# One meeting of the engines between six stages instead of two, with the finished stage's semaphores cleared inside the next stage and Pool's queue not drained

## What is computed

```
x = x + 0.5 * moe(layernorm(x))          # 8 experts, the best 2 of each token, hidden width 256
x = x + attention(layernorm(x))          # 16 heads of 16, rotary, causal softmax
x = x + 0.5 * moe(layernorm(x))          # the same weights again
x = x + 0.5 * hadamard_ffn(layernorm(x)) # fwht(silu(x W1) * (x W3)) W2, hidden width 1024
x = x + feature_attention(layernorm(x))  # sin and cos of random projections in place of the softmax
x = x + 0.5 * hadamard_ffn(layernorm(x))
```

## Time and profile before

| | us |
|---|---|
| median of 3 runs | 1163.23 |
| the runs | 1161.66 to 1166.33 |
| span of the profiled execution | 1142.1 |
| median less span | 21.1 |

### The profile page before, as it was taken

One profiled execution on the slowest core, in us unless ns is written; L12 is line 12 of the kernel. 1 busy time (PEld: TensorE's weight loads), 2 busy tenths in 40 slices (PEclk: granted clock), 3 DMA queues, 4 the chain that ended last, 5 costly groups with the idle time before them and its releaser, 6 DMA issues. The chain is left out here.

```text
span 1142.1 us, 18339 instructions
## 1 busy us (share of the span) xinstructions
PE 1029.9 (90%) x6327; PEld 844.4 (74%) x6327; DVE 732.0 (64%) x1755; ACT 449.2 (39%) x768; POOL 430.7 (38%) x473
## 2 busy tenths in 40 slices
PE   4889995879999999978999987999988998899997
PEld 3778884756566655568878886888877987788886
DVE  7935442899788876647454445756648978456654
ACT  4324331327576654525343322232325543232222
POOL 3046663337363721203556531000129987300000
PEclk8689998889899997896999998999998999999999
DMA  9024422400000010119452241000010120000000
GB/s 335 37 74 139 171 88 83 128 0 2 2 2 20 2 39 20 39 37 352 149 189 89 79 174 53 1 1 1 1 74 1 28 47 1 1 1 19 20 19 19
DMA packets 39339, 72.49 MB, mean 63 GB/s; under 512 B 10642, under 2 KB 28114, under 8 KB 38996
## 3 DMA queue, kind: packets, MB, share of 16 engines
q1 hardware_dynamic: 29460, 48.25, 12.6%
q0 software_dynamic: 7680, 20.98, 5.6%
q10 hardware_dynamic: 2112, 2.10, 0.5%
HBM read 47.04 MB, written 24.13 MB: 62 GB/s over the span
## 5 line engine op out<-in xcount | busy, mean ns | idle before, releaser
L2139 PE MATMUL ps<-xt,w 128*128 128x512 f32 x768 | 191.3, 399 | 7.5 <-PEq L66 7.5
L2139 PEld LDWEIGHTS ps<-xt,w 128*128 128x128 f32 x768 | 142.4, 191 | 37.0 <-issue 5.8
L1822 DVE CUSTOM_DVE_ANT_0 ps<-ps,att_mask 128x128 f32<-128x128 f32 (+3 forms) x256 | 119.2, 515 | 27.2 <-PE ps L1371 26.9
L717 PE MATMUL ps<-moe_w,moe_narrow_xb 128*128 x480 | 127.6, 402 | 0.0
L2233 DVE TENSOR_TENSOR had_gated<-ps,had_sig 128x512 f32<-128x512 f32 x64 | 44.2, 691 | 109.7 <-ACT had_sig L2192 109.7
L2192 ACT ACTIVATE had_sig<-ps 128x512 f32<-128x512 f32 x64 | 38.2, 597 | 188.4 <-PE ps L2139 188.4
L1679 ACT ACTIVATE att_early_probs<-ps 128x384 f32<-128x384 f32 (+1 forms) x192 | 91.2, 528 | 52.1 <-PE ps L1386 51.5
L122 POOL TENSOR_TENSOR var_eps<-bn,eps 128x4 f32<-128x4 f32 x24 | 6.6, 274 | 277.0 <-DVE bn L99 263.0
L621 POOL DMA_INDIRECT made_rows<-moe_units_made,moe_index x80 | 79.4, 993 | 80.4 <-ACT moe_units_made L844 68.3
L615 POOL DMA_INDIRECT moe_xs<-xn_rows,moe_index x80 | 79.3, 991 | 76.0 <-DVE moe_index L1016 44.1
L717 PEld LDWEIGHTS ps<-moe_w,moe_narrow_xb 128*128 128x128 f32 x480 | 92.0, 192 | 20.2
(11 more groups left out here) (286 smaller groups left out, 2242.8 us busy)
## 6 DMA issues: line engine op xcount, KB each, us to landing
moe_w<-in_moe SPq DMA_DIRECT2D x16, 768.0 KB, 8.9
back<-made_rows SPq DMA_DIRECT2D x16, 512.0 KB, 5.4
x<-x_turned SPq DMA_DIRECT2D x8, 512.0 KB, 8.6
low_weights<-moe_w SPq DMA_DIRECT2D x4, 768.0 KB, 3.6
moe_w<-low_weights SPq DMA_DIRECT2D x4, 768.0 KB, 15.2
x<-in_x SPq DMA_DIRECT2D x4, 512.0 KB, 5.5
xn_rows<-moe_wide_xn SPq DMA_DIRECT2D x4, 512.0 KB, 10.6
moe_narrow_later<-in_w SPq DMA_DIRECT2D x4, 512.0 KB, 4.6
```

Source lines behind the costliest of these rows:

```text
L717: last = nc.tensor.matmul(h_bank(j, i), xb[a][:, j % 2, i, k, :], weight(c), start=False, stop=(k == KC - 1 and c == 1))
L1822: last = nc.vector.tensor_tensor_reduce(g.ps[:, a, col:col + n], g.ps[:, a, col:col + n], mask[:, SEQ - n:SEQ], -1.0, 3.0e38, ALU.add, ALU ...
L2139: last = nc.tensor.matmul(g.ps[:, bank(n, half), :], w[a][:, k, c * P:(c + 1) * P], xt[low][:, b % 2, k, :], start=(k == 0 and q == 0), st ...
```

## The change

A stage no longer clears its semaphores when it ends. It hands the list on, and the next stage has it cleared by Pool after the one meeting that is left, ahead of Pool's list of that stage. That list is allocated while the old one is still held, so semaphores which only one of the two experts stages uses are now made in that one alone. `no_gpsimd_drain=True` takes Pool's own drain out of the meeting. In had0 Pool waits for its two weight subtractions before it leaves the stage. After the last stage nothing is cleared.

```
 class Semaphores:
+    finished = []
     def __init__(self, nc, ctx, tag):
         self.nc, self.tag, self.held = nc, tag, []
-        ctx.callback(self.clear)
+        ctx.callback(self.hand_on)
...
-    def clear(self):
-        self.nc.clear_and_free_semaphores(self.held)
-        self.nc.all_engine_barrier()
+    def hand_on(self):
+        Semaphores.finished.append(self.held)
+
+    def clear_finished(self):
+        while Semaphores.finished:
+            self.nc.clear_and_free_semaphores(Semaphores.finished.pop())
...
         # in each of the four stage functions
-        block = ctx.enter_context(nc.Block())
+        sem.clear_finished()
+        block = ctx.enter_context(nc.Block(no_gpsimd_drain=True))
...
         # hadamard_stage, Pool's list
-                    nc.gpsimd.tensor_tensor(w[1][:, :, :], raw[:, :, :], f32(w[0][:, :, :]), ALU.subtract)
+                    nc.gpsimd.tensor_tensor(w[1][:, :, :], raw[:, :, :], f32(w[0][:, :, :]), ALU.subtract) \
+                        .then_inc(raw_low, 1)
+                pool.wait_ge(raw_low, 2)
```

More of the change, by code:

```diff
@@ L464, in experts_stage @@
         later = narrow("later", [P, HID])
-        consts, small_here, b2_here = sem("consts"), sem("small_here"), sem("b2_here")
+        b2_here = sem("b2_here")
+        if which == 0:
+            consts, small_here, xn_stored, pool_const = sem("consts"), sem("small_here"), sem("xn_stored"), sem("pool_const")
         x_here = [sem(f"x_here{b}") for b in range(BATCH)]
         rec_here = [sem(f"rec_here{e}") for e in range(E)]
-        low_here = [sem(f"low_here{e}") for e in range(E)]
-        low_stored = sem("low_stored")
+        if which == 1:
+            low_here = [sem(f"low_here{e}") for e in range(E)]
+        if which == 0:
+            low_stored = sem("low_stored")
         LOADED = E // 2 if which == 1 else 0
         b1_here, b1_filled = sem("b1_here"), sem("b1_filled")
[L473 to L476, removed]
+        hi_split, lo_split, zeroed = sem("hi_split"), sem("lo_split"), sem("zeroed")
+        if which == 0:
+            gate_split, both_done = sem("gate_split"), sem("both_done")
+        if which == 1:
+            route_turned, rows_out, rows_stored, route_here = (
+                sem("route_turned"), sem("rows_out"), sem("rows_stored"), sem("route_here"))
         routed, margin_done, route_done, chosen_done = (
@@ L481, in experts_stage @@
         b1_turned, b_hi, b_row = sem("b1_turned"), sem("b_hi"), sem("b_row")
-        xn_stored = sem("xn_stored")
         gathered = [sem(f"gathered{s}") for s in range(AHEAD)]
@@ L501, in experts_stage @@
             jobs += split(g.w1, "w1")
-        w3_here, w3_hi, mixed, w2_hi = sem("w3_here"), sem("w3_hi"), sem("mixed"), sem("w2_hi")
+        if which == 1:
+            w3_here, w3_hi, mixed, w2_hi = sem("w3_here"), sem("w3_hi"), sem("mixed"), sem("w2_hi")
         later_here, later_hi, later_lo = sem("later_here"), sem("later_hi"), sem("later_lo")
@@ L2050, in hadamard_stage @@
             raws = [sb("lqkv_raw", [P, KC, 2 * D]), sb("lout_raw", [P, KC, D])]
-        raw_here, raw_hi = sem("raw_here"), sem("raw_hi")
+        raw_here, raw_hi, raw_low = sem("raw_here"), sem("raw_hi"), sem("raw_low")
         rope_here, bias_here, blocks_here = sem("rope_here"), sem("bias_here"), sem("blocks_here")
```

## The result

The changed kernel takes 1157.38 us (median of 12 runs, 1155.20 to 1161.63); the kernel before 1165.11, in 12 runs too. The ratio is 0.9940, with a 95% interval from 0.9922 to 0.9958: 7.0 us less, and 4.9 to 9.1 by the interval. The forecast time of 1157.5 us was met, but in part by luck: the gain was forecast as 5.7 us against a median of 1163.23, and its main assumption, a long drain behind the meeting, did not hold.

The account below looks back on a forecast made before the run. PE, busy for 90% of the span, bounds most of a stage, so only seams could move. Terms of 0.6 + 0.9 + 2.9 + 0.5 + 0.5 + 0.5 - 0.2 = 5.7 us off 1163.2 gave 1157.5 us, range 1153.8 to 1161.5.

Parts of the forecast that it names:

- The second meeting: At each seam, dropping it saves 1.1, 0.9, 1.0, 0.5, 0.5 us, fea to had1 taken at 0.5; 0.2 off for six meetings.
- Pool's drain: Behind moe0 and moe1: 6.6 us after Pool's last work, expected to move behind the meeting into the clear's drain.
- the prediction's own signs: At att's start: wrong if the drain is short or grows; Pool's first memset expected some 7 us behind the release.
- the second rival: At att's start: the clear's drain takes only 0.2 us, gain there 2.2 us, time 1155.9 us; chance 0.15.
- a fixed piece of work: Behind the experts stages: the first drain after software DMAs does 6.6 us of it once Pool stands idle.
- moe1 to had0: Seam into had0: engines go on at 690.5 instead of 693.4, gain 2.9 us; Pool's later return stays hidden.
- moe0 to att: Seam into att: release at 194.6 instead of 199.6, but Pool's long drain delays its norm; gain only 0.6 us.
- The clock's rival: At had0's start: PE's low clock costs 2.5 us more (1160.0, chance 0.13) or stays at 1.00 (1155.0, chance 0.07).
- The sum: Over all seams and the end: 0.6 + 0.9 + 2.9 + 0.5 + 0.5 + 0.5 - 0.2 = 5.7 us.

## Why the prediction was right, and where it was not

**The second meeting** was sized rightly. Forecast 0.9, 0.5, 0.5 and 0.5 us for the four seams without a long drain, less 0.2 for the instruction that adds to the semaphore; measured 0.82, 0.43, 0.52 and 0.39 to 0.42, with that instruction in it; it costs 0.07 to 0.09 us a meeting by the run with the drain kept, so some 0.3 for these four.

**Pool's drain is the step that failed:** "So the 6.6 us is not removed; it moves behind the meeting, onto Pool alone." The clear's own drain took 0.17 us. I had argued that it would become the first drain behind the software DMAs and do their work. It does become the first, but it is of another kind, behind which a plain drain finds nothing left to do (the run with the two kinds in a row). By the prediction's own signs this made it wrong: the drain was short, and Pool's memset did not come 7 us behind the release. So the second rival held, that the clear's drain is short because it is of another kind. I had given it 0.15, and the row I held against it, that L65's drains came right behind a full one, says nothing on their kind. That the 6.6 us were "a fixed piece of work" was wrong too: they go with the number of DMAs, 0.083 us for each of 80.

That the 6.6 us are not transfers in flight, which the prediction read from SP's two rows, held: a plain drain still took 6.59 us when it began 18.7 us behind the last scatter.

**moe1 to had0** came as worked out: forecast 2.9, measured 2.89 (3.24 to 0.35). With the short drain Pool's work was hardly later at all (its norm at 721.7 waited 13.5 us). That a long one is hidden there too, as the prediction said, the run with the plain drain behind the meeting shows: the same 0.35, and the norm still waits 6.3 us for DVE.

**moe0 to att** is the term that was mis-sized with it: forecast 0.6, measured 1.3 to 1.6. The working itself stands: with the long drain put behind the meeting the seam is 20.48, 0.3 to 0.6 below before, Pool's norm ends 13.1 us behind the release at 206.27 (13.1 forecast, 207.7 - 194.6), and PE's projections start 17.6 behind it (17.7 forecast). SP waits for Pool's first memset there, as forecast (214.38 against 213.62 + 0.74). In the kernel before it did not: that memset was done at 200.4, and SP came to the bias row at 203.53; nor does it in the changed kernel. Without the drain the prediction had 2.2, and 0.6 to 0.9 of that did not come. The bias row is loaded 2.8 us behind the release, where it was 4.0 (209.90 - 207.06 against 203.53 - 199.57), so DVE makes it as soon as its statistics are done, from 217.10 to 218.04, and Pool's norm operation, which in its usual 0.19 us would have finished at 216.9, ends at 218.09. Moved behind the normalise it costs that no longer; the seam is then 18.25, 2.6 to 2.9 below before, more than the 2.2. The load was late before because one of SP's issues ahead of it took 1.35 to 1.63 us in the three profiles whose meeting held Pool's drain, and 0.43 in the nine others; why is open. Pool's operation began ahead of DVE's, at 216.69 against 217.10, and ended 0.05 us behind it, 1.40 us long. That the two collide is read from the lengths alone, 1.40 us in six profiles and 0.19 to 0.20 in six; how DVE's operation holds up one that began 0.41 us earlier, no run here explains.

**The clock's rival** did not happen in either direction: 0.50 over the same 5.1 us, and the first 36 products in 11.00 us against 10.98. The stop was 2.7 us instead of 5.6, and the clock fell all the same, within it and ahead of the release: it is 1.00 up to 704.6, 0.57 in 704.6 to 705.0 and 0.50 from there to the release, with a mean of 0.71 over the stop. With PE at work up to 0.7 us ahead of had0 it stays at 1.00. No trace gives this clock in GHz, only as a share of full speed. The prediction's 1.2 agrees with what the 12 products at 0.50 took (512 columns in 5.1 / 12 = 0.425 us, 1.2 a nanosecond); its 2.4 is twice that by the share alone, as the 22 products at 1.00 took 5.1 / 22 = 0.232 us each, 2.2 a nanosecond.

**The sum:** 5.7 forecast, 6.3 to 6.7 read from the seams. **The time** was met to within 0.2 us by luck: the median of before over 12 runs is 1165.11, 1.9 above the 1163.23 of three runs that I subtracted from, and the gain came out larger by about as much, since what the short drain gave back was only in part lost to the bias row. The forecast for the short drain, 1155.9, missed by 1.5 us although its mechanism was the right one. That I took 21.1 us as lying around the span, where 1.7 do, did no harm, because every term was a difference within a seam, made against the median.

## What to carry over

Two instructions with one name can do different work: before a cost is said to move, find a run in which the second instruction meets the state that the first one met. A seam is best measured from the last engine's drain to the next stage's first work, where it repeats to a tenth of a microsecond, when the stages around it vary by ten. And an edit that makes a load earlier also makes what waits for it earlier, so look for what it will then run beside.

## What the runs showed of the hardware

On an idle Pool a plain drain behind software DMAs takes 0.083 us for each DMA issued since the last drain (3.15 us for 38, 6.60 for 80), 2.9 us behind the last of them as well as 18.7; inside the loop it took longer than that. The drain that goes with a clear of semaphores took 0.14 to 0.20 us right behind 80 DMAs, and a plain one behind it 0.04 to 0.19. Two profiles of one kernel differed by 11 us in moe0 and by 13 in moe1; in the long one PE waits for the turned tiles, and why they are late stays open.
